# Placing a pair's slot operations behind the attention contexts on VectorE, in a fused convolution, attention and expert-choice kernel

## What is computed

```python
x = conv_block(x)                       # 16 images of 256 x 14 x 14; 1x1, 3x3, 1x1 convolutions, batch norms, residual
t = to_tokens(x)                        # [16, 196, 256]
t = t + attention(layer_norm(t))        # linear attention: q softmax over 16 channels, k softmax over tokens
h = layer_norm(t)
probs = softmax(h @ gate_w + gate_b)    # 8 experts
top_p, top_i = top_k(probs, 2)
comb = scatter(top_p / (sum(top_p) + 1e-9))
out = t + sum_e comb[:, e] * (gelu(h @ w1[e] + b1[e]) @ w2[e] + b2[e])
```

## Time and profile before

| what | value |
|---|---|
| median of three runs | 687.7 us (687.45, 687.7, 690.37) |
| the profiled execution, its own time | 689.3 us |
| its span | 687.4 us |
| mean granted TensorE clock | 0.947 |
| busy share of the span: PE, DVE, ACT, POOL | 90%, 66%, 46%, 32% |
| chain that ended last: PE, DVE | 69%, 20% |
| the steps of the pipeline, as read from the timeline | even steps 10, 12, 14, 16 have their L1312 at 154.1, 177.2, 200.2 and 221.8 us |
| the 56 tiles of the experts | from about 284 us to the end |

### The profile page before, as it was taken

How to read it: one execution, slowest core, us unless ns; L and a number is a source line. 1 busy time by engine, 2 the same in 40 slices (tenths; PEclk the granted TensorE clock), 3 DMA queues, 4 the chain that set the end, 5 groups by cost and what they waited for, 6 DMA issues and landing times.

```text
span 687.4 us, 13862 instructions
## 1 busy us (share of the span) xinstructions
PE 616.8 (90%) x3960; PEld 546.7 (80%) x3960; DVE 455.4 (66%) x1472; ACT 319.2 (46%) x624; POOL 218.5 (32%) x194
## 2 busy tenths in 40 slices
PE   7984799989999974489999999999999999999982
PEld 3862678878788864379999999999999999999971
DVE  2877899999998886346565655556565655656550
ACT  0575788888785522133334333333334333333430
POOL 7041233315656667502112222222121222212120
PEclk9996899999999985599999999999999999999995
DMA  9718999888959953422383745626528337222211
GB/s 247 239 62 306 361 351 326 302 293 302 353 201 361 355 182 92 132 45 38 73 289 49 232 131 162 200 44 196 171 35 291 76 99 256 48 44 37 32 17 16
DMA packets 50198, 121.10 MB, mean 176 GB/s; under 512 B 7309, under 2 KB 38865, under 8 KB 43985
## 3 DMA queue, kind: packets, MB, share of 16 engines
q1 hardware_dynamic: 30368, 98.54, 39.8%
q0 software_dynamic: 11136, 14.00, 12.0%
q10 hardware_dynamic: 8624, 7.68, 4.2%
HBM read 68.09 MB, written 52.11 MB: 175 GB/s over the span
## 4 chain that ended last, share of the span: by engine, by line
PE 69%; DVE 20%; issue 4%; ACT 2%; POOL 2%; DMA 1%; DVEq 1%; SPq 0%; ACTq 0%; POOLq 0%
PE ps L947 46%; PE ps L974 7%; DVE wset L1225 3%; DVE stt L1134 2%; PE ps L740 2%; PE ps L722 2%; PE ps L796 2%; PE ps L940 2%; PE ps L751 2%; PE ps L785 1%; PE ps L847 1%; POOL rows_by_expert L456 1%; DVE tc L1125 1%; DVE img L1219 1%; DVE cT L1211 1%
## 5 line engine op out<-in xcount | busy, mean ns | idle before, releaser
L478 POOL DMA_INDIRECT out<-ys,xr x56 | 86.7, 1548 | 302.4 <-DVE ys L1548 220.5
L947 PE MATMUL ps<-wset,hTh 128*128 x896 | 162.7, 282 | 3.4 <-DVE hTl L1516 3.4
L947 PE MATMUL ps<-wset,xrTh 128*128 x448 | 148.7, 414 | 1.2 <-DVE xrTl L1522 1.2
L947 PEld LDWEIGHTS ps<-wset,hTh 128*128 128x128 f32 x896 | 141.6, 190 | 9.7 <-issue 4.8
L677 ACT ACTIVATE hb<-hb 128x512 f32<-128x512 f32 x112 | 70.3, 633 | 138.4 <-DVE hb L1537 133.0
L947 PE MATMUL ps<-wset,hTl 128*128 x448 | 126.1, 281 | 0.0
L683 ACT CAST hTh<-ps 128x512 fp32r<-128x512 f32 x112 | 60.2, 590 | 99.4 <-PE ps L974 99.4
L1543 DVE TENSOR_TENSOR yb<-ps,bset 128x256 f32<-128x256 f32 x56 | 23.8, 425 | 124.5 <-PE ps L947 124.5
L947 PEld LDWEIGHTS ps<-wset,xrTh 128*128 128x128 f32 x448 | 82.0, 193 | 17.7 <-issue 1.6
L947 PE MATMUL ps<-wset,xrTl 128*128 x224 | 90.2, 403 | 0.0
L1537 DVE TENSOR_TENSOR hb<-ps,bset 128x512 f32<-128x512 f32 x112 | 75.4, 684 | 19.7 <-PE ps L947 19.6
(11 more groups left out here) (199 smaller groups left out, 945.8 us busy)
## 6 DMA issues: line engine op xcount, KB each, us to landing
split_weights<-wset SPq DMA_DIRECT2D x16, 2048.0 KB, 7.4
wset<-split_weights SPq DMA_DIRECT2D x32, 1024.0 KB
wset<-in_ew SPq DMA_DIRECT2D x16, 1024.0 KB, 10.5
xr<-rows_by_expert ACTq DMA_DIRECT2D x56, 132.5 KB, 2.3
bset<-in_eb SPq DMA_DIRECT2D x8, 640.0 KB
out<-img SPq DMA_DIRECT2D x16, 196.0 KB
img<-in_x SPq DMA_DIRECT2D x6, 392.0 KB, 7.2
rows_by_expert<-padrow SPq DMA_DIRECT2D x9, 132.5 KB, 3.3
```

The lines of the kernel that those rows point to most:

```text
L478: pool.indirect_dma_start(out, bass.IndirectOffsetOnAxis(xr[:, r % XR, C + E:ROW].bitcast(U32), 0), ys[:, r % YS, :], None, compute_op=ALU ...
L947: last = pe.matmul(dst, rows_k[:, k * 128:(k + 1) * 128], wset[:, bass.ds(column(k) + rest, width)], start=(k == 0 and n == 0), stop=(k == ...
```

## The change

In the even steps the slot operations of the pair before are no longer put between the roots. They are issued behind the contexts, in turn with the three operations of `route_choose`, and all seven come ahead of the matrix subtraction.

```diff
                 if on["in"]:
                     in_mix(i["in"])
-                if n % 2 == 0 and g >= 1:
-                    chains[1] = route_slots(g - 1)
                 for _ in chains[0]:
                     next(chains[1], None)
                 if on["ctx"]:
                     ctx_ctx(i["ctx"])
                     fill()
                 if n % 2 == 0 and pair:
-                    for _ in chains[1]:
-                        pass
                     chains[1] = route_choose(g)
+                    if g >= 1:
+                        for _ in route_slots(g - 1):
+                            next(chains[1], None)
                     fill()
                 if EARLY <= n - 1 + EARLY < UNITS:
                     split_rest(n - 1 + EARLY)
```

## The result

| what | before | after |
|---|---|---|
| median of 7 runs each | 688.06 us (687.45 to 690.37) | 692.36 us (690.73 to 693.39) |
| profiled execution, its span | 689.3 us, 687.4 us | 691.46 us, 689.6 us |

The ratio is 1.005, with a 95% interval of 1.0031 to 1.0069: 2.1 to 4.7 us slower, where I had forecast 1.45 us, and the median lies above my range of 687.2 to 691.2 us.

A forecast was written before the change was run, and what follows sets the result against it. DVE was taken to bound steps 8 to 15; +0.71 - 0.25 = +0.46 us a step (step 14 +0.53) made 1.45 us over three steps, so 687.7 + 1.45 = 689.1 us, range 687.2 to 691.2 us.

The forecast's parts named there:

- What bounds the stage: Steps 8 to 15: DVE is the bound, and its delay by 211 us is handed to PE in full.
- The seven operations: Behind the contexts in even steps: L1225 starts 0.71 us later, in step 14 0.78 us.
- the sums: L1196 to the next statistics in even steps, without L1254 and L1257: gives back 0.25 us.
- the roots: Even steps without slot operations: last root 0.11 us earlier, counted as nothing because L1211 goes by PE's product.
- (a): Rival, position is free: roots' gain real, seven operations at 0.55 us, whole +0.3 us, 688.0 us; 10%.
- (b): Rival, faster through ACT: the exponential's 0.58 us comes back in three steps, 686.0 or 685.6 us; 6%.
- (d): Rival, each DVE operation waits for the one before to end: seven take 1.3 to 1.6 us, 690.9 us; 4%.
- Step 16 at nothing: Step 16: statistics 0.53 us later, covered by L1265's 1.14 us wait for the exponential; costs nothing, uncovered 0.5 us.
- ACT's matrix cast and the three copies behind it move forward by 0.58 us: ACT's exponential no longer waits for L1257, PE gets the values earlier in the odd step; costed at nothing.
- Rival (c), POOL's port: Odd steps' routing: a two-operand DVE operation falls into POOL's L438, +1.0 us in each of three steps, 692.1 us; 6%.
- a stretch of lower granted clock: A stretch of lower granted clock that the shifted waits could bring on, no place or size given; 3%.

The follow-up runs named there:

- after_look1: The changed kernel unchanged, run once more for a second trace; measured 691.24 us.
- exp_late: The changed kernel, but ACT's exponential of an even step waits again, for DVE's reciprocal of the key sums; 691.84 us, ratio 1.0057.
- delay_only: The kernel before with nothing moved, one DVE reduction of 384 elements added ahead of L1225 in steps 10, 12 and 14; 691.63 us, ratio 1.0042.
- choice_early: The kernel before with all three choice operations ahead of the subtraction, the slot operations still between the roots; 691.09 us, ratio 1.0052.
- slots_alone: The changed kernel, but choice operations L1254 and L1257 stay behind the subtraction as before; 693.07 us, ratio 1.0078.
- spares_tail: The kernel before with 30 spare PE products in PE's long wait for the experts' first rows; 689.58 us, ratio 1.0011.
- spares_before: The kernel before with four spare PE products in each of steps 11, 13 and 15, as a control; 692.39 us, ratio 1.005.
- spares_odd: The changed kernel with four spare PE products in steps 11, 13 and 15, one ahead of L806, three ahead of L822; 688.95 us, ratio 1.0013.

## Why the prediction was wrong

- **What bounds the stage.** Right. DVE was the bound from step 10 to 15, its lateness reached step 15 in full, and from step 17 on all moved with it.
- **The seven operations, the sums, the roots.** Right to 0.01 us each, and the sum of three steps, 1.45 us, was measured as 1.47 and 1.44. With it rivals (a), (b) and (d) are out: the seven took 0.80 to 0.87 us, neither 0.55 nor 1.4, and nothing came back through ACT.
- **Step 16 at nothing.** Right: L1265 of step 17 still waits for the exponential, 0.44 us in after_look1 where it was 1.14 us, and the two steps take 20.40 us in the trace in which no clock fell there.
- **"ACT's matrix cast and the three copies behind it move forward by 0.58 us ... I cost this at nothing."** This is the step that failed, and with it the same silence about DVE's lateness: I asked what idle PE delays (nothing) and not how fast PE runs behind its waits, so the sum has no term for PE's clock. In step 15 the waits of PE were 0.38 + 0.74 us before and became 0.92 + 0.74; in step 13 the 0.80 us ahead of the values and 0.26 ahead of L822 became 0.50 + 0.74 close together. The clock went to its lower level behind them in one step of each of the three traces of the changed kernel, at a cost of 1.5 to 1.7 us, more than the 1.45 us that I had priced. The earlier values are not what it needs: it fell in exp_late and in delay_only too.
- **Rival (c), POOL's port.** It did not happen, and that its 692.1 us lies near the measured 692.4 is chance. POOL was pushed, as worked out: its L432 of step 12 lasted 2.76 us, which is the 1.54 us until DVE's operation behind L1225 started at 182.79, and 1.22, about the 1.27 us that L432 takes in step 16, without an L1225 beside it. L438 ended at 185.02, and L1282 came at 186.29. The Trainium skill's rule of the shared port ("SBUF — State Buffer", section "Who interferes with whom") is borne out by this lengthening of L432. It cost nothing that steps 9 to 15 show, since DVE's own 1.45 us account for all of their delay.
- **The 3% for "a stretch of lower granted clock".** It was this case. It had neither a place nor a price, and so no fair chance. The rows to price it were at hand: PE's two waits ahead of the context product of step 15, and L822 at 1.42 us in the tail, where the clock falls in the kernel before.

This much is shown: with DVE later in the even steps (the change, choice_early, exp_late, delay_only, slots_alone) PE's waits ahead of L806 and L822 of step 15 are longer, and in 6 of 10 traces the clock falls behind these two waits, in step 13 or 15, at a cost of 1.5 to 1.7 us. In the kernel before it fell in 0 of 3, and in 0 of 1 of spares_tail, which is the same up to step 17.

That the longer waits bring the fall is the likeliest reading, and is not shown. The fall doesn't get more frequent with them: in step 15 it came in 3 of 4 traces with 1.3 to 1.7 us of waits (choice_early and the change) and in 2 of 6 with 1.8 to 1.9 us (exp_late, delay_only and slots_alone). With spares in the waits ahead of L822 it came in 0 of 4, but there the medians and mean clocks of spares_before speak the other way. Open are also why one execution of a program has the fall and another has none, the last 1.0 us between the medians, and the two groups of spares_odd.

## What to carry to other kernels

In a stage that one engine bounds, TensorE's waits may have a price of their own: here they grew by about half a microsecond, and a stretch at the lower clock behind them cost as much again as the 1.45 us that were added on VectorE. So when an edit makes another engine later, or feeds TensorE earlier, list its waits in the steps that follow and price a stretch at the lower clock as a rival with a place. And take more than one trace of a kernel before a difference of a few microseconds is read from it: stage by stage these traces agree to 0.05 us, and in the stages where the clock moves they differ by 1 to 3 us.

## What the runs showed of the hardware that I had not expected

The fall came without a long pause: behind waits of 0.50 and 0.74 us, with 0.64 us of transposes between, PE ran at 1.2 GHz for about 3.5 us, and lost 1.7 us on L822 and L785 together. The Trainium skill, page "TensorE: Matmul & The Clock Gate", section "Part 1: The HAM clock gate", says that the chip sets this clock by how busy PE has been; the traces agree as far as they go: every fall in steps 9 to 17 follows two waits of PE, and with the waits filled the clock stayed at 1.00 in both traces of spares_odd. They also show that equal waits do not always bring it: in delay_only it fell behind 1.15 + 0.73 us in one trace, and not behind 1.15 + 0.74 in the other.
